# The high parts of a feed-forward layer are cast by ScalarE in place of VectorE, with new order tables

## What is computed

```python
x = x + attn_a(layernorm(x))
x = x + ffn(layernorm(x))
x = x + attn_b(layernorm(x))
x = x + ffn(layernorm(x))

def ffn(x, ...):                       # w1, w2: (1024, 256), h1, h2: (1024, 1024), w3: (256, 1024)
    h = silu(x @ w1.T * w1_s) * (x @ w2.T * w2_s)
    h = gelu(h @ h1.T * h1_s)
    h = gelu(h @ h2.T * h2_s)
    return h @ w3.T * w3_s
```

## Time and profile before

| | us |
|---|---|
| median of 3 runs | 2490.34 (2489.7 to 2496.93) |
| profiled execution | 2494.62 |
| span of the profiled execution | 2492.6 |

### The profile page before, as it was taken

How to read it: one execution, slowest core, us unless ns; L and a number is a source line. 1 busy time by engine, 2 the same in 40 slices (tenths; PEclk the granted TensorE clock), 3 DMA queues, 4 the chain that set the end, 5 groups by cost and what they waited for, 6 DMA issues and landing times.

```text
span 2492.6 us, 60186 instructions
## 1 busy us (share of the span) xinstructions
PE 2245.7 (90%) x24704; PEld 1963.5 (79%) x24704; DVE 1221.2 (49%) x3186; ACT 1102.8 (44%) x2169; POOL 804.7 (32%) x873
## 2 busy tenths in 40 slices
PE   5798985897999989999999989999899999899888
PEld 3577974676888878887788878888798888888788
DVE  4546344455635654355534656346543655434431
ACT  3465431363435733365333654356342664333233
POOL 3222331322333233332333333332332333233233
PEclk8799997898999999999999999999999999999999
DMA  8000001000010001000010000100010000000000
GB/s 258 1 1 1 1 6 29 4 1 3 17 36 2 1 11 39 7 1 2 19 34 4 1 2 18 36 2 1 7 40 10 1 1 18 25 4 19 18 11 9
DMA packets 85456, 43.69 MB, mean 18 GB/s; under 512 B 69936, under 2 KB 80048, under 8 KB 85168
## 3 DMA queue, kind: packets, MB, share of 16 engines
q1 hardware_dynamic: 81504, 28.11, 4.6%
q0 software_dynamic: 3664, 11.53, 1.4%
HBM read 27.05 MB, written 12.58 MB: 16 GB/s over the span
## 4 chain that ended last, share of the span: by engine, by line
PE 55%; issue 16%; DVE 14%; POOL 9%; ACT 3%; DMA 1%; SPq 0%; DVEq 0%; POOLq 0%; ACTq 0%
PE F L1336 23%; PE Q L1395 5%; PE F L1315 5%; POOL hA_lo L604 4%; PE Q L1465 2%; PE F L1358 2%; PE Q L1429 2%; DVE hid L976 2%; POOL hB_lo L604 2%; PE Q L1448 2%; POOL rn L660 2%; DVE Q L1176 2%; DVE ti L1178 2%; PE Q L1433 1%; PE Q L1407 1%
## 5 line engine op out<-in xcount | busy, mean ns | idle before, releaser
L604 POOL TENSOR_TENSOR hA_lo<-hid,hA_hi 128x512 fp32r<-128x512 f32 x256 | 333.4, 1303 | 660.4 <-ACT hA_hi L741 348.0
L1336 PE MATMUL F<-hB_hi,h_sb 128*128 128x256 f32 x2048 | 499.7, 286 | 6.4 <-POOL hB_lo L604 6.4
L1336 PE MATMUL F<-hA_hi,h_sb 128*128 128x256 f32 x2048 | 500.8, 287 | 4.2 <-POOL hA_lo L604 4.2
L1336 PE MATMUL F<-hA_lo,h_sb 128*128 128x256 f32 x2048 | 487.5, 280 | 4.8 <-issue 4.8
L1336 PE MATMUL F<-hB_lo,h_sb 128*128 128x256 f32 x2048 | 488.4, 280 | 0.0
L1336 PEld LDWEIGHTS F<-hB_hi,h_sb 128*128 128x128 f32 x2048 | 387.2, 189 | 16.1 <-POOL hB_lo L604 8.8
L1336 PEld LDWEIGHTS F<-hA_hi,h_sb 128*128 128x128 f32 x2048 | 386.5, 189 | 13.2 <-POOL hA_lo L604 6.4
L1336 PEld LDWEIGHTS F<-hA_lo,h_sb 128*128 128x128 f32 x2048 | 387.1, 189 | 6.9 <-issue 6.6
L1336 PEld LDWEIGHTS F<-hB_lo,h_sb 128*128 128x128 f32 x2048 | 387.9, 189 | 0.0
L1315 PE MATMUL F<-xf_hi,w_sb 128*128 128x256 f32 x1024 | 275.3, 305 | 39.3 <-DVEq L980 21.0
L737 ACT ACTIVATE hid<-F,sh_sb 128x256 f32<-128x256 f32 x256 | 121.7, 475 | 392.2 <-PE F L1336 382.7
(11 more groups left out here) (199 smaller groups left out, 3953.8 us busy)
## 6 DMA issues: line engine op xcount, KB each, us to landing
h_sb<-h_dram POOLq DMA_DIRECT2D x2, 4096.0 KB, 23.8
x_sb<-x_dram SPq DMA_DIRECT2D x8, 512.0 KB, 5.5
a_scr<-amv SPq DMA_DIRECT2D x32, 128.0 KB, 2.3
au<-a_scr SPq DMA_DIRECT2D x8, 512.0 KB, 3.2
t_scr<-ti SPq DMA_DIRECT2D x8, 512.0 KB, 2.6
tbd<-t_scr SPq DMA_DIRECT2D x128, 32.0 KB, 1.9
out_dram<-x_sb SPq DMA_DIRECT2D x8, 512.0 KB, 3.0
w_sb<-w_dram POOLq DMA_DIRECT2D x3, 1024.0 KB, 7.8
```

The source lines that it names most:

```text
L604: pool.tensor_tensor(lo, hid[:, n % 2], hi.bitcast(F32), ALU.subtract).then_inc(f_lo.handle, 1)
L1336: last = pe.matmul(ps[:, i * TOK:(i + 1) * TOK], w[:, k, o:o + P], part[:, k, :], start=(i == 0 and k == 0 and part is src[0]), stop=(i == ...
```

## The change

In layer 1 the cast to the high part leaves VectorE and goes to ScalarE. It does not stand directly behind VectorE's products: ScalarE casts pair m-1 right behind the second silu of pair m, which has already waited for VectorE's products of pair m-1. For the last pair there is one new step of ScalarE with a wait for VectorE (`f_freeV`), ahead of the first gelu. GpSimd still waits for `f_hi`, which ScalarE now raises. No other instruction is added or removed.

All twenty tables are new. Below are those that are spoken of further on; what they amount to there is:
- first window: more of h1 and h2 stands between the steps of the scan's tiles 4 to 6 (between scores and sums, and ahead of the segment products);
- second window, TensorE: between the last gram matmuls and the walk stand 10 half slices in place of 8;
- loop, GpSimd: it opens with the clearing of `ti` and the first inverse norm, and then come the first two low parts, where one low part stood first; the third inverse norm stands ahead of the third low part, no longer behind it. ScalarE (table not shown): in the third tile its squares and tanh stand between the last two silus of the first unit;
- loop, TensorE: 30 feed-forward steps in place of 32 at the longest stretch, the last before the walk;
- LATE, VectorE: layer 1 of the second unit has one inversion step between two pairs of products, where there were up to three;
- LAST, VectorE: the making of `xnf` stands ahead of the first inversion step, where it was behind 15 of them; TensorE: 28 steps in place of 26 and, around the walk, more ahead of it and fewer in it.

```diff
@@ -63,49 +63,49 @@
...
 FIRST_PLAN = {
-    "pe": ("0 0 0 0 0 0 0 0 0 0 0 0 0 0 0 0 0 0 0 0 0 0 0 0 0 1 0 1 1 1 2 0 2 0 0 1 1 2 0 1 0 0 0 0 0 0 3 0 "
-             "3 0 2 0 0 1 2 2 0 2 0 0 0 1 1 3 4 5 0 7 1 2 6 3 21"),
...
+    "pe": ("0 0 0 0 0 0 0 0 0 0 0 0 0 0 0 0 0 0 0 0 0 0 0 0 0 0 1 1 3 1 0 1 1 0 0 2 1 3 0 1 0 1 0 0 1 0 2 0 "
+             "1 0 1 0 0 1 0 3 0 0 2 2 2 0 4 1 3 10 1 1 0 2 19 5 5"),
...
 PEEL_PLAN = {
-    "pe": ("2 0 0 2 0 1 0 0 0 0 1 1 2 5 0 0 8 0 0 0 0 0 0 0 0 0 0 0 0 0 0 0 0 0 0 0 0 1 0 0 0 0 0 0 3 0 0 0 "
-             "0 0 1 4 1 0 1 4 3 0 2 0 2 0 0 0 1 0 3 0 0 0 1 0 0 0 0 2 0 0 1 0 0 0 0 0 0 0 0 0 0 0 2 0 0"),
...
+    "pe": ("2 0 0 1 0 1 1 0 0 2 2 0 0 1 0 1 10 0 0 0 0 0 0 0 0 0 1 0 0 0 1 0 0 0 0 0 0 0 0 0 0 0 0 0 1 0 2 "
+             "0 1 2 0 0 2 1 3 0 5 0 1 2 0 2 0 0 0 0 2 0 0 0 0 0 0 0 1 2 0 0 0 0 0 0 1 1 0 0 1 0 0 0 1 0 0"),
...
 BODY_PLAN = {
-    "pe": ("2 0 3 0 0 1 1 0 0 0 1 1 0 0 2 1 32 1 0 0 1 0 0 0 0 1 0 1 0 0 2 1 1 0 0 3 2 1 0 0 2 0 2 0 0 2 1 "
-             "0 0 0 1 2 1 2 1 2 3 1 0 8 2 0 0 0 2 0 4 0 1 0 0 1 0 2 0 3 0 0 0 0 0 0 1 0 3 0 1 0 0 1 1 0 0"),
...
-    "pool": ("1 0 1 1 1 13 4 4 2 2 1 1 3 1 1 5 0 3 2 0 2 0 0 1 0 1 2 0 0 0"),
+    "pe": ("2 0 1 2 0 2 0 0 0 1 0 1 0 0 2 1 30 1 1 1 1 0 2 0 0 1 1 1 0 0 1 0 1 2 0 1 1 1 0 0 1 1 2 0 0 4 1 "
+             "1 0 0 1 0 1 1 1 2 3 1 0 8 0 1 2 1 1 0 4 0 1 0 0 0 0 1 0 4 0 0 0 0 0 0 1 0 3 0 1 0 0 1 1 0 0"),
...
+    "pool": ("0 0 2 0 2 14 7 0 1 4 2 1 2 0 0 5 3 0 0 1 3 1 0 1 2 0 1 0 0 0"),
...
 LATE_PLAN = {
...
-    "dve": ("0 3 1 2 1 1 0 0 2 5 0 0 0 0 0 0 0 0 0 0 0 0 0 0 1 0 1 1 2 1 0 3 0 2 0 0 0 0 0 1 0 1 0 0 2 0 0 2 "
-             "0 0 1 0 0 0 0 0 0 0 0 0 1 1 0 0 1 0 2 1 0 1 0 4 0 0 0 0 1 1 0 0 0 0 1 0 7"),
...
+    "dve": ("1 4 1 1 0 1 0 1 2 0 0 0 0 1 0 0 1 2 1 0 0 0 0 0 0 0 1 0 4 1 2 1 3 0 1 0 0 1 0 1 0 1 0 0 0 0 0 0 "
+             "0 1 0 0 1 0 0 0 0 0 0 1 0 0 2 1 0 3 0 0 1 0 0 2 0 1 0 1 1 0 1 0 0 0 1 2 3"),
...
 LAST_PLAN = {
-    "pe": ("3 1 3 0 1 2 0 0 0 2 0 0 0 2 1 0 26 1 0 0 1 0 0 0 0 0 0 3 0 0 0 0 1 0 0 0 0 0 0 0 1 0 0 0 0 2 0 "
-             "0 0 0 0 0 2 0 1 0 1"),
...
-    "dve": ("2 3 1 2 0 0 0 2 0 0 0 0 0 2 0 0 0 0 1 0 0 0 0 0 0 0 1 0 2 0 0 0 0 0 2 3 2 2 0 1 0 0 0 0 0 0 0 0 "
-             "0 0 0 0 0 1 0 1 0 0 0 0 2 0 0 0 1 0 0 1 0 0 0 0 0 0 0 0 2 0 0 0 0 0 0 2 0"),
...
+    "pe": ("3 1 2 1 0 2 1 1 1 1 0 1 0 1 1 1 28 0 0 0 1 0 0 0 0 0 0 0 0 0 0 0 0 0 0 1 0 0 0 0 1 0 0 0 0 1 0 "
+             "0 0 0 1 0 1 0 1 0 2"),
...
+    "dve": ("2 3 1 3 0 2 0 1 0 0 1 1 0 2 0 0 0 0 0 0 0 0 0 0 1 0 4 2 1 1 2 0 0 2 0 0 0 0 0 0 0 0 0 0 0 0 0 0 "
+             "0 0 0 0 0 0 0 0 0 0 1 0 0 0 1 0 1 0 0 0 0 0 0 0 0 0 0 1 0 0 0 0 1 0 1 0 1"),
...
@@ -712,6 +712,10 @@
                 act.wait_ge(f_ps.handle, f_ps.at(p, s + 1))
                 act.copy(xf_hi[:].rearrange("p t k n -> p (t k n)"), bank_of(s)[:]).then_inc(f_xhi.handle, 1)
 
+            def high_part(p, u, m):
+
+                act.copy(ffn_dst(m)[0], hid[:, (u * DONE + m) % 2]).then_inc(f_hi.handle, 1)
+
             def ffn(p, b, more=True, units=range(UNITS)):
                 for u in units:
                     s0 = u * SLICES
@@ -725,6 +729,12 @@
                             act.wait_ge(f_freeV.handle, f_freeV.at(p, u * (KP + 2) + m))
                         act.activation(gate[:, i, :], bank_of(s0 + 2 * m)[:, i * TOK:(i + 1) * TOK], ACT.Silu,
                                        scale=s1_sb[:, j:j + 1]).then_inc(f_act.handle, 1)
+                        if i and m:
+                            high_part(p, u, m - 1)
+                    yield s0 + KT - 0.4
+
+                    act.wait_ge(f_freeV.handle, f_freeV.at(p, u * (KP + 2) + KP))
+                    high_part(p, u, KP - 1)
                     for j in range(KP, DONE):
                         n = u * DONE + j
                         s = s0 + KP + j
@@ -978,7 +988,6 @@
                                                              s2_sb[:, 2 * m + i:2 * m + i + 1], gate[:, i, :],
                                                              ALU.mult, ALU.mult))
                             dve.sem_inc(f_freeV.handle, 1)
-                            dve.tensor_copy(ffn_dst(m)[0], hid[:, n % 2]).then_inc(f_hi.handle, 1)
                         if j == HSLICES - 2:
                             if u + 1 < UNITS:
                                 norm_unit(p, x, u + 1, 1 if final else 0)
```

## The result

| | before | after |
|---|---|---|
| median, us | 2493.64 (2489.7 to 2501.45, 4 runs) | 2469.66 (2466.47 to 2471.75, 4 runs) |
| ratio | | 0.9899, 95% interval 0.987 to 0.9928 |
| span of the profiled execution, us | 2492.6 | 2467.4 |

The account below looks back on a forecast made before the run. TensorE, busy 90% of the span and 55% of the last chain, was taken as the bound. Terms +1.4 + 2.5 - 5 - 4 - 4 - 3.1 - 0.4 = -12.6 us took 2490.3 to 2478 us; range 2456 to 2503.

Parts of the forecast that it names:

- The cast in a bare unit: Loop units with no attention step between layer 1 and h1's start: late cast loses 0.27 us each, x5 = +1.4 us.
- The other bare units: Five units outside the loop, no attention step between layer 1 and h1's start: cast costs 0.5 us each, +2.5 us.
- The first unit of a pass: Loop: GpSimd's clearing and masking moved ahead of the first low part let TensorE go on 1.5 us earlier; -5 us in all.
- net -1.0 us a pass: Loop's first unit: 1.5 us gained, against one half of 0.9 us for a late low part; x5 = -5 us.
- The first window: Kernel's start: new tables fill about half of TensorE's 8.0 us of `seg` waits, -4 us; bounds -8 - 3.3 and +4.
- The second window: Ten half slices in place of 8 between last gram matmul and walk: -3.7 us, with cover in the walk -4.
- wait for `tbd`: Second window: TensorE's wait for the inverse, 16.34 us before, would be near 12.6 us.
- LATE: Window after the loop: one inversion step between product pairs saves 1.4 us, half clock gone 1.7 more; -3.1 us.
- LAST: Last window: `xnf` earlier gives -3.5 and -1.7 us, lost walk cover +2.3 and lower clock +2.5; -0.4 us.
- The moved work only shifts the waits: Rival: first window and first units of passes give nothing back; 2487 us, chance 0.27.
- The late low part decides: Rival: late low part stalls h1's first slice for pair 2, clock falls, other units lose too; 2505 us, chance 0.17.
- The loop gains more: Rival: `uw` wait goes in all passes, free-bank waits shrink, 5 us a pass; 2457 us, chance 0.14.

Follow-up runs that it names:

- e2: Changed kernel with all twenty new tables but the cast still on VectorE; 2498.82 us, ratio 1.0023 to the kernel before.
- e11: The changed kernel itself, run again beside the same runs of the kernel before, for comparison with e10; 2468.35 us, ratio 0.9896.
- e1: Kernel before with the cast moved to ScalarE, old tables except small order changes to keep engines from waiting in a ring; 2563.49 us, ratio 1.0289.
- e4: Changed kernel with the last window's tables of before, the cast's new ScalarE step added; 2475.13 us, ratio 0.9933.
- e6: Kernel before with GpSimd's clearing and masking of `ti` and first inverse norm ahead of its first low part in the loop; 2493.96 us, ratio 0.9987.
- e10: e7 with one more wait: in the loop GpSimd's first low part waits for VectorE's `uw` of the first tile; 2457.82 us, ratio 0.9845.
- e8: Changed kernel with ScalarE's cast of a pair ahead of both silus of the next pair, tables unchanged; 2478.39 us, ratio 0.9923.
- e3: Kernel before with only the first window's four tables new, cast on VectorE; 2482.33 us, ratio 0.9967.
- e9: Kernel before with two TensorE layer 1 steps moved ahead of tile 3's segment product in the first window; 2499.4 us, ratio 1.0013.
- e12: e9 with VectorE's first pair of products also moved ahead of `seg` of tile 3; 2493.6 us, ratio 1.0003.
- e7: e5 with the GpSimd order of e6 in the loop; 2465.36 us, ratio 0.9872.
- e5: Changed kernel with the loop, the last window and the last two units taken back, both tables and cast; 2473.37 us, ratio 0.9898.

## Why the prediction was right, and where it was not

**The cast in a bare unit: right.** The low part of pair 2 is later, TensorE waits twice, 0.58 + 0.18 against 0.47 before: +0.29 us, forecast +0.27. The first of the two was to be 0.9: the low part ends 2.70 us behind the start of the silus (946.35 to 949.05), where I had 2.87, as the cast starts ahead of the silus' listed end. The layer 1 period stays (2.61 us, before 0.84 + 1.79 = 2.63). The other bare units were put at +0.5 each, but the two at the end take 97.4 us, 2.4 less than before. That is the doing of the LAST tables: with them these units take 97.2 us with VectorE's cast (e2) and 97.4 and 97.7 with ScalarE's (after, e11); with the old ones 99.8 to 100.3 and 100.8 (e1, e4). At equal tables the cast costs 0.2 to 1.0 us for both, so the +1.0 of the forecast was the upper end.

**The first unit of a pass: the wait was sized well, its price in the kernel was not.** The norm starts 0.09 us behind `srow`, and the 2.16 us wait is wholly gone; I had said 1.5. But the step "net -1.0 us a pass" counted only one thing against it, the late low part at half of 0.9 us. The wait is 1.23 us in that unit, and GpSimd's third norm ahead of the low part makes it, not the cast (e2). `xnd` (5.3 us in the loop) and `hat` (5.1) were not in the sum at all. Nor were the 12 more changes of work a pass, x 0.11 = 1.3 us. My reason for the gain, the masking moved ahead, was also only part of it: alone (e6) it gives 0.5 us of the wait. With the collision taken away as well 1.55 us of it are gone (e10), and in the changed kernel it is ScalarE's late cast that keeps the low part away from VectorE's product (e2, e8). The last 0.6 us come with the rest of the new order. I had used that very mechanism for `xnd` (1.49 us beside the masking) and did not ask what would stand beside `k_sb` next. The Trainium skill ("SBUF — State Buffer", "SBUF: two separate sides") gives the rule: a VectorE instruction with two SBUF inputs and a GpSimd instruction that reads SBUF hold one port pair by turns, each for its whole length. e6 (1.48 us) and e10 (0.42 us) agree.

**The first window: the term that made the result.** Forecast -4, bound -11.3, measured -19.4, of which 15.7 lie behind the first layer 1 matmul. There TensorE's idle time falls by 6.5 us (18.8 to 12.3), within the 8.0 that the forecast counted. The failed step is the clock's share: I took none of it in the -4 and a tenth, 3.3 us, in the bound. TensorE's busy time for the same matmuls falls by 9.2 us (215.93 to 206.75), and what half clock took by 10.2 (11.9 to 1.7). Of the 33 us that I took the tenth of, about 20 lie ahead of that matmul, where the tables change next to nothing; I had not asked where they lay. Half clock takes 1.7 to 5.1 us in this stretch in the seven kernels with both changes, 5.1 and 8.5 with the tables alone (e2, e3), and 6.8 to 11.9 in the five with the first window as it was or nearly so. What a wait and what the half clock behind it are worth is not parted by an experiment of its own.

**The second window: right in size, wrong in place.** The wait for `tbd` was to be 12.6 us:

```profile
390.00 1.08 PE L1533 MATMUL Q<-tbd,uw 128*32 128x128 f32 x16 [19.04 <-DMA tbd<-t_scr]
```

It is 19.04, against 16.34 + 3.59 = 19.93 before. The chain from the last gram matmul takes 38.4 us, 1.6 more than before (36.8), and TensorE's clock is at half from 374.9 to 409.1. The part of the gain that can be named is the wait for `seg` in the scan behind it, 11.2 to 6.8 us. The size itself is loosely known: the same kernel took 257.8 us in this window in another profile (e11), with 8.5 us less of half clock.

**LATE: right** (-2.5 against -2.6), and e2 gives the same 181.0 without the cast: the tables' doing. **LAST: the wrong sign.** The 3.5 us wait for `xnf` went as said, and the walk lost cover as said; its price was too low. Half clock took 10.2 us in LAST in place of 3.4, 5.1 of them by one stretch in the walk:

```profile
2330.80:2341.00 10.20, 7.77 (x165) 6.05 (x155) 3.25 (x11) 0.38 (x1) 0.81 (x2) 0.50 0.08 13
```

The forecast allowed 2.5 us for that. All four kernels with the new LAST tables have such a stretch of 10.2 us at 0.50 in the walk, with either engine's cast (after, e2, e8, e11); none of the others has one over 7 us in LAST. Still the whole term is small against the spread: with VectorE's cast the old tables gave 145.5 to 150.5 us, and the new ones gave 148.6 to 151.8.

**The rivals.** *The moved work only shifts the waits* is what the loop does, and what e9 and e12 do; it was right for 59% of the kernel. *The late low part decides* did not come: the stall of 0.58 us leaves the clock alone. It is not far off, though: with the old tables the same lateness makes 70 us (e1). *The loop gains more* is refuted. That the total fell into the range is in part luck: a gain put at a fifth of its size in one window (4 of 19.4 us) stood beside two terms that were 4 us too kind each, the loop and LAST.

## What to carry to other kernels

Behind an in-order queue, ask of a delayed signal not only who reads it but what stands behind the waiting instruction on its reader's engine: here the reader lost 0.3 us a unit, and the chain behind it 4 us a pass (e1). A cast moved to another engine and the order tables made for it are one change: each alone was slower or nothing. Of a new order, count the changes between kinds of work on the busiest engine; they cost as much as the waits saved in the loop. And look for gains window by window: this change's gain lies in windows that make up under a third of the kernel, and leaving the loop nearly as it was and placing one wait gave 10 us more.

## What the runs showed of the hardware

- VectorE's `k_sb` product, 0.42 us alone, took 1.48 us when a GpSimd subtraction had started 0.06 us before it. It took 1.48 to 1.51 us in the first tile of all five passes in four kernels where the subtraction stood there (e2, e6, e7, e8), and one wait on GpSimd gave the time back (e10).
- A feed-forward matmul behind a change between two kinds of work takes 0.37 to 0.39 us (0.28 within one), also where no wait is listed; 12 changes a pass more cost the loop about as much as the idle time it saved.
- One code of a loop lost 5.1 to 18.3 us to half clock in different kernels around it (e3, e5; both have the loop of before). The same kernel, profiled twice, lost 37.5 and 29.0 us in its second window (after, e11). A difference of under 10 us between two single profiles says little without this number.
